# Transposing the last tile ahead of the second layer, and moving one fold, in a recommendation kernel

## What is computed

```python
emb = embed_table[f_ix, x_idx]                       # n, 26, 16
lin1 = w1_table[f_ix, x_idx].sum(axis=1, keepdims=True) + w1_bias
s = emb.sum(axis=1)
fm = 0.5 * ((s * s).sum(-1) - (emb * emb).sum(axis=(1, 2)))[:, None]
h = emb.reshape(n, F * D)
h = relu(h @ mlp_w1 + mlp_b1)                        # first layer, 416 x 400
h = relu(h @ mlp_w2 + mlp_b2)                        # second layer, 400 x 400
deepfm_result = lin1 + fm + h @ mlp_w3 + mlp_b3
x0 = emb.transpose(0, 2, 1)
last, feats = x0, []
for W in (cin_w0, cin_w1, cin_w2):
    last = einsum('ndl,ndf,klf->ndk', last, x0, W)
    feats.append(last)
cin_result = concatenate(feats, -1).sum(axis=1) @ lin_w + lin_b
return deepfm_result + cin_result
```

## Time and profile before

| | |
|---|---|
| median of 3 runs | 497.66 us (497.53 to 498.18) |
| profiled execution | 496.48 us, its span 494.7 us |
| PE busy | 453.1 us, 92% |
| DVE busy | 414.2 us, 84% |
| ACT busy | 368.2 us, 74% |
| POOL busy | 345.5 us, 70% |
| granted TensorE clock, mean | 0.991 of full speed |

### The profile page before, as it was taken

How to read it: one execution, slowest core, us unless ns; L and a number is a source line. 1 busy time by engine, 2 the same in 40 slices (tenths; PEclk the granted TensorE clock), 3 DMA queues, 4 the chain that set the end, 5 groups by cost and what they waited for, 6 DMA issues and landing times.

```text
span 494.7 us, 6809 instructions
## 1 busy us (share of the span) xinstructions
PE 453.1 (92%) x2171; PEld 383.0 (77%) x2171; DVE 414.2 (84%) x861; ACT 368.2 (74%) x726; POOL 345.5 (70%) x365
## 2 busy tenths in 40 slices
PE   0988986899999999999999999999999999999898
PEld 0985764788888888888888888888877887878666
DVE  6163358999999999999999999999989989989676
ACT  0163499678787887888787878787887878687694
POOL 5777778777777777777777777777777777777000
PEclk9999998899999999999999999999999999999999
DMA  7963794222222222222222222222222222222000
GB/s 159 209 168 27 110 201 113 38 7 8 8 9 7 7 9 7 10 7 8 8 8 7 8 8 8 7 8 8 8 8 9 7 9 7 8 8 7 3 0 2
DMA packets 21522, 15.59 MB, mean 32 GB/s; under 512 B 12802, under 2 KB 19823, under 8 KB 21359
## 3 DMA queue, kind: packets, MB, share of 16 engines
q0 software_dynamic: 11520, 3.16, 18.6%
q1 hardware_dynamic: 6962, 9.99, 8.2%
q10 hardware_dynamic: 3005, 2.01, 2.0%
HBM read 14.92 MB, written 0.21 MB: 31 GB/s over the span
## 4 chain that ended last, share of the span: by engine, by line
POOL 65%; issue 22%; ACT 5%; PE 4%; DVE 3%; DMA 1%; POOLq 0%; DVEq 0%
POOL emb L499 65%; ACT ps_s L598 2%; ACT z_hi L591 2%; ACT z_hi L593 1%; DVE z_lo L796 1%; PE ps_q L1096 1%; PE ps_y L1127 1%; DVE xt L789 0%; DMA idx_raw<-x_idx 0%; PE ps_q L1097 0%; PE ps_q L1098 0%; DMA emb<-rows,idx_raw 0%; ACT room_a L597 0%; DVE sums L822 0%; DVE ps_y L935 0%
## 5 line engine op out<-in xcount | busy, mean ns | idle before, releaser
L499 POOL DMA_INDIRECT emb<-rows,idx_raw x360 | 345.1, 959 | 112.2 <-issue 109.4
L796 DVE TENSOR_TENSOR z_lo<-ps_s,z_hi 128x512 fp32r<-128x512 f32 (+1 forms) x192 | 131.4, 684 | 35.0 <-ACT ps_s L598 34.4
L591 ACT ACTIVATE z_hi<-ps_s 128x512 fp32r<-128x512 f32 (+1 forms) x192 | 114.4, 596 | 40.3 <-PE ps_s L1083 39.9
L598 ACT ACTIVATE ps_s<-ps_s 128x512 f32<-128x512 f32 (+1 forms) x192 | 113.9, 593 | 0.8
L1182 PE MATMUL ps_y<-look_hi,one_hot 128*128 128x442 f32 x224 | 82.1, 366 | 6.4 <-DVE one_hot L924 5.7
L1083 PE MATMUL ps_s<-xt,pick 128*128 128x512 f32 (+1 forms) x192 | 77.2, 405 | 9.3 <-ACT x_two L584 6.6
L1096 PE MATMUL ps_q<-z_lo,zw_hi 128*127 128x512 f32 (+1 forms) x192 | 79.6, 415 | 6.6 <-DVE z_lo L796 4.8
L1183 PE MATMUL ps_y<-look_lo,one_hot 128*128 128x442 f32 x224 | 79.4, 356 | 0.0
L1098 PE MATMUL ps_q<-z_hi,zw_hi 128*127 128x512 f32 (+1 forms) x192 | 75.9, 395 | 0.0
L1097 PE MATMUL ps_q<-z_hi,zw_lo 128*127 128x512 f32 (+1 forms) x192 | 75.8, 395 | 0.0
L1083 PEld LDWEIGHTS ps_s<-xt,pick 128*128 128x128 f32 (+1 forms) x192 | 35.6, 186 | 23.4 <-DVE z_lo L796 11.2
(11 more groups left out here) (187 smaller groups left out, 687.3 us busy)
## 6 DMA issues: line engine op xcount, KB each, us to landing
emb<-rows,idx_raw POOLq DMA_INDIRECT x360, 3.0
w_space<-rows SPq DMA_DIRECT2D x2, 728.9 KB
m_space<-rows SPq DMA_DIRECT2D x2, 728.9 KB
w_space<-key_scratch SPq DMA_DIRECT2D x1, 1408.0 KB, 8.6
w<-cin_w SPq DMA_DIRECT2D x2, 416.0 KB, 6.7
w<-cin_w ACTq DMA_DIRECT2D x2, 416.0 KB, 9.3
w_space<-cin_w SPq DMA_DIRECT2D x2, 416.0 KB, 8.4
w_space<-cin_w ACTq DMA_DIRECT2D x2, 416.0 KB, 8.2
```

Of the source, the lines that this page charges most:

```text
L499: pool.indirect_dma_start(emb[t % EMB][:, f, :], None, rows, bass.IndirectOffsetOnAxis(row_ix[:, t, f:f + 1], 0)).then_inc(gathered[t] if ...
L591: act.activation(z_hi[0:k, c, :], ps[0:k, :], ACT.Square)
L598: act.activation(ps[0:k, :], ps[0:k, :], ACT.Square).then_inc(hi_ready, 1)
L796: z = dve.tensor_tensor(z_lo[0:k, u % NC, :], ps, z_hi[0:k, u % NC, :].bitcast(F32), ALU.subtract)
```

## The change

There are two parts.

**The fold.** `fold(t - 1)` stood at the end of DVE's `start_tile(t)`, ahead of unit 3 of tile t. It now stands behind `z_low` of unit 4. With it, PE's `sum_products(t - 1)` goes from behind unit 3 to behind unit 6, and the number of look-ups for which it waits goes up by one. In the last tile the fold stays at the end of `start_last`.

**The start of the last tile.** On PE `x_all(15)` now comes ahead of `hidden2(14)`, and the eight discarded products and the wait in front of them are gone. On ACT `copy_last_early` stands ahead of `square(14, 11)` and no longer behind it. On DVE `start_last` has a new order.

```diff
             def looked_by(t):
-            return min(max(LOOKS * t + 1 - LATER, 0), look_no(T, 0))
+            return min(max(LOOKS * t + 2 - LATER, 0), look_no(T, 0))
...
                     if u == NU - 2 and t + 1 < T - 1:
                         copy_by_position(t + 1)
+                    if u == NU - 1 and t + 1 == T - 1:
+                        copy_last_early()
                     square(t, u)
                     if u == NU - 1 and t + 1 == T - 1:
-                        copy_last_early()
                         copy_last_late()
...
                     if u % NC == 2 and q:
                         add_product(t, q)
+                    if u == 4 and 0 < t < T - 1:
+                        fold(t - 1)
...
             def start_last():
                 t = T - 1
+                times_third(t - 1)
                 times_left(t - 1, NQ - 1)
-                times_third(t - 1)
-                add_third(t - 1)
-                hidden2(t - 1)
                 x_low(t, 0)
                 x_low(t, 1)
                 z_low(t, 0)
+                hidden2(t - 1)
+                add_third(t - 1)
                 z_low(t, 1)
...
                 add_product(t - 1, NQ - 1)
-                fold(t - 1)
...
-                    if u == 3 and t:
+                    if u == 6 and t:
                         sum_products(t - 1)
...
                 else:
+                    x_all(after)
                     hidden2(t)
-                    wait_for_bank(after, 1)
-                    free = s_bank(after, 0)
-                    keep_warm(free, WARM_LAST[0])
-                    x_all(after)
-                    keep_warm(free, WARM_LAST[1])
                     picked(after, 0)
```

More of the change, by code:

```diff
@@ L376, in deepfm_cin_kernel @@
         CONSTS = 10
-        WARM, WARM_FIRST, WARM_LAST = 8, 4, (4, 4)
+        WARM, WARM_FIRST = 8, 4
         MOVES = [3 + 2, 2 + 2, 1 + 2]
```

## The result

The changed kernel takes **498.86 us** in the median of 15 executions (496.98 to 500.2); the kernel before, run beside it, takes 497.64 us (15 executions, 496.67 to 498.18). The ratio is 1.0025, with a 95% interval of 1.0014 to 1.0036. Run a second time, it came out at 1.0015 (1.0004 to 1.0025). So it is slower by 0.8 to 1.2 us, and its executions lie further apart, where I forecast 0.3 us less. A ratio here can differ from that of the two medians by up to 0.0007. Three executions of 630 to 1096 us (two of the kernel before, one of e13) are left out.

What follows compares the result with a forecast made beforehand. POOL's gathers were taken to set the pace up to tile 14's copy, ACT after it. Of 0.69 + 1.7 us won, some 2.1 are given back, leaving 0.3: 497.66 to 497.4 us, range 496.4 to 499.2.

Steps and rivals of the forecast that it cites:

- the look-up: Tile 14 on PE: with the fold moved, the look-up starts at 450.36, 0.69 us earlier.
- the transposes: Passage to tile 15 on PE: transposes start at 463.8 where they were at 466.20, 2.4 us earlier.
- unit 0 on ACT: Start of tile 15: ACT's unit 0 at 466.5 against 468.79, 2.3 us earlier.
- `hidden2(14)`: Start of tile 15 on DVE: standing behind unit 0, it starts at 468.8 and takes 0.57 us.
- PE's idle time: Ahead of tile 15's first layer, PE idles some 2.8 us for DVE; some 2.1 us of the gain is given back.
- the two terms of the sum: Tile 14 and last tile: 0.69 us from the fold, 1.7 from earlier transposes; 0.3 left at unit 2.
- rival A: PE's clock falls in the 2.8 us idle stretch at 466.6 to 469.4: 498.7 us, up to 500.2; chance 0.33.
- tiles 0 to 13 are worth nothing either way: Before tile 14's copy at 432.93, loop gains only lengthen waits for gathers; up to 3.7 us may be lost unseen.
- Rival B: The wait at hidden1_whole(15) does not bind, unit 0's 2.3 us are kept: 495.3 us, halfway 496.5; chance 0.12.
- Rival C: Gathers hold tile 14 or the copies later and the fold is worth nothing: 498.0 to 498.1 us; chance 0.08.

Runs made afterwards that it cites:

- e13: e3 with the one-hot matrix made by a tensor_tensor comparison in place of tensor_scalar; ratio 0.9999 to the kernel before.
- e3: Kernel before with only the fold moved behind unit 4 and sum_products behind unit 6, last tile's start unchanged; 496.3 against 496.99 us, ratio 0.9990.
- e2: Changed kernel with 14 discarded products on PE ahead of the wait for hidden2(14); 496.87 us against 496.99 for the kernel before, ratio 0.9997.
- e7: Kernel before with one gather left out in each of tiles 4 to 14; 492.75 against 497.24 us, ratio 0.9918.
- after: The changed kernel itself, with both parts of the change; 498.86 us, ratio 1.0025 to the kernel before.
- e10: e4's kernel run again, on the same chip as e9; ratio 1.0032 to the kernel before, 498.61 us.
- e4: Changed kernel with the fold and sum_products back at their old places, so only the last tile's start is changed; ratio 1.0014 to the kernel before.
- e8: e3 with one gather left out in each of tiles 4 to 14; 488.51 us, ratio 0.9831 to the kernel before.
- e14: Kernel before with DVE's one-hot matrices left out from the third look-up on (wrong rows picked); one execution, 495.61 us beside 496.94.
- e15: e3 with DVE's one-hot matrices left out from the third look-up on (wrong rows picked); one execution, 495.67 us beside 496.94.
- e6: Kernel before without the eight discarded products and the wait for a bank; 496.83 against 497.24 us, ratio 0.9992.
- e9: Changed kernel run again, unaltered; ratio 1.0015 to the kernel before, 497.96 us.
- e1: Changed kernel with hidden2(14) moved ahead of unit 0 on DVE in start_last; 495.23 us against 496.99 for the kernel before, ratio 0.9959.
- e12: Kernel before with the one-hot matrix made by a tensor_tensor comparison in place of tensor_scalar; ratio 1.0009.
- e11: e5 with the one-hot matrix made by a tensor_tensor comparison in place of tensor_scalar; ratio 0.9950 to the kernel before.
- e5: e1 with copy_last_early put back behind unit 11 of tile 14; 494.69 us against 497.24 for the kernel before, ratio 0.9951.

## Why the prediction was wrong

**Right, by the trace.** Every step up to the idle stretch came where it was put, shifted by 1.73: the look-up at 450.36 (450.36 forecast), the transposes at 463.7 (463.8), unit 0 on ACT at 466.4 (466.5), `hidden2(14)` at 468.75 (468.8), PE's idle time 2.75 us (2.8). e3 and e2 measure the two terms of the sum by themselves: 0.74 for the fold (0.69), and 0.45 for both parts at full clock (0.3).

**The step that failed first is the choice between the forecast and rival A.** I gave "the clock falls" 0.33 and took the full clock. The row that should have decided it was there: the fall behind 81.59 in the earlier trace rows came with shorter idle stretches than 2.8. Against it I held that the 1.64 us stretch had no fall. That was the luck of one record. The same stretch stands in all traces near 64 us, and in two of the sixteen where the clock was high ahead of it (e7 and e13) it fell there; e7's rows, and the stretch behind them (columns as in the earlier trace rows):

```profile
63.48 0.71 PE L1096 MATMUL ps_q<-z_lo,zw_hi 128*127 128x512 f32 x1 [1.64 <-DVE zw_lo L979]
```

```profile
64.00:66.00 2.00, 2.00 (x6) 1.61 (x5) 0.69 (x1) 1.19 (x5) 1.70 (x2) 0.50 1.13 251
```

Behind the 1.84 us stretch (1.84 to 1.89 in the traces) it fell in all seventeen, and behind 2.75 us in three of four. Its price was in order: 1.3 forecast, 0.7 (e2 against after) to 1.46 (e10 against e4) measured. The half-clock stretch in the last tile lasted about 3.4 us, not the 6.8 of the earlier trace rows. The time lies inside the range; sign and likeliest case were wrong.

**The second is "tiles 0 to 13 are worth nothing either way".** That what the loop gains is waited away is right (e7, e8). But I took the gathers' own times as fixed. They depend on what DVE does beside them (e14, e15), and moving work on DVE seems to change how much they are held up. Of the 2.0 us between the two profiled executions, 1.73 lie there. The 73rd gather already starts 0.72 later (98.15 before, 98.87 after), and that looks like chance: with the fold at its old place it starts at 98.85 to 99.12 in e4, e6 and e12. The other 1.09 arose behind 100 us, where the means above give the change some 0.6.

**The sum then reads**: 0.45 gained in the passage and the fold at full clock, 0.7 to 1.5 lost to the low clock in an execution with a fall, and at most some 0.6 to later gathers. For such an execution that is up to +0.85 to +1.65; measured are +0.8 and +1.2 in the median. The size of the gathers' share stays open: e3's median keeps 0.7 of the 0.74 in its tail, which leaves little room for it.

In what share of executions the clock falls stays open too, but not without a sign. The mean granted clock is on record for each. Over the 49 executions that leave the wait unfilled (after, e4, e9, e10) it is 0.987, and 17 of them have 0.986 or less. Over 88 of the kernel before it is 0.991, with one such, and over the 33 of e2, e3 and e6 also 0.991, with none. A single execution can't be sorted by it, since the start has falls of its own; the profiled one after the change has the low clock from about 55.8 to 69.4 us as well.

**Rival B** (the wait does not bind) was wrong as a forecast, but its price was right: with the wait nearly gone, e1's tail is 2.36 shorter, where 2.4 stood in the text. **Rival C** (the fold worth nothing) is refuted by the tails of e3 and of e13 beside e12, and by e8 beside e7.

## What to carry to other kernels

When an order is changed, follow every semaphore that the moved step releases: here one step of 0.57 us, put behind two others on DVE, held PE for 2.75 us though DVE had 1.1 us idle just ahead of those two. A new idle stretch of PE longer than one behind which the trace already shows a fall should be priced at the lower clock as the likeliest case, and either closed (e1) or filled (e2). One trace in which the clock held behind such a stretch does not show that it will hold. And where an engine with a fixed pace sets the loop, ask what disturbs that pace, not only who waits for it.

## What the runs showed of the hardware

- **A DVE instruction holds up an indirect gather of POOL beside it.** With all gathers and the `tensor_scalar` form, 7 to 15 gathers behind 100 us take 0.98 to 1.18 us in place of 0.94, each beside a one-hot instruction of 128 x 128 (keys of 16 bits in SBUF against a column of numbers); without it, none. The Trainium skill, "SBUF — State Buffer", section "Who interferes with whom", says that DVE shares a pair of SBUF ports with GpSimd and that `tensor_scalar` in its two-port modes blocks it. The overlaps fit that; in which mode the instruction ran no run here shows. For `tensor_tensor` with both inputs in SBUF the same section of the Trainium skill says that it contends with GpSimd's reads, and infers that descriptor generation is not held up. e11 and e13 have gathers of 1.65 and 1.67 us beside it, so the gather is held up with this form too; which part of it, no run here shows.
- **The clock falls in some executions of the same kernel and not in others** behind the same idle stretch of PE: behind 2.75 us in e4 and not in e10, behind 1.64 us in two traces of sixteen, of versions that are alike up to there. Behind 1.84 to 1.89 us it fell in all seventeen, behind a stretch of 2.23 to 2.27 us between 94 and 100 us in all five that have one (after, e5, e6, e11, e12), and behind 1.49 us in e6 it stayed. These stretches have other idle time near them, so the runs give no length that is safe.
- **Discarded products can keep the clock** (e2: 14 of them, mean clocks of 0.990 to 0.992 where the changed kernel has 0.975 to 0.991), and be of no use where the stretch is short (e6).
